# Where the inverse of a softmax row sum is taken: GpSimd's power operation or VectorE's reciprocal

## The reference

```
xn  = layernorm(x)
q,k,v = xn @ Wq + bq, xn @ Wk + bk, xn @ Wv + bv        (16 heads of 128; q as a reshape of the projection)
w   = softmax(q k^T / sqrt(128) + causal mask)
out = x + (w v) @ Wo + bo + ffn(xn)
```

## Time and profile before

| | us |
|---|---|
| median of 3 runs | 1319.09 (1319.01 to 1320.17) |
| profiled execution, its own time | 1319.28 |
| its span, first to last instruction | 1317.0 |
| TensorE busy | 1232.1 (94%) |
| TensorE weight load busy | 1072.9 (81%) |
| VectorE busy | 947.8 (72%) |
| GpSimd busy | 795.8 (60%) |
| ScalarE busy | 766.3 (58%) |

### The profile page before, as it was taken

One profiled execution on the slowest core, in us unless ns is written; L12 is line 12 of the kernel. 1 busy time (PEld: TensorE's weight loads), 2 busy tenths in 40 slices (PEclk: granted clock), 3 DMA queues, 4 the chain that ended last, 5 costly groups with the idle time before them and its releaser, 6 DMA issues.

```text
span 1317.0 us, 20858 instructions
## 1 busy us (share of the span) xinstructions
PE 1232.1 (94%) x7468; PEld 1072.9 (81%) x7468; DVE 947.8 (72%) x1734; ACT 766.3 (58%) x1575; POOL 795.8 (60%) x799
## 2 busy tenths in 40 slices
PE   3799999999899999999999999999999999999997
PEld 2677777777678888888888988898888878889886
DVE  7778877888676667676766677767666776667666
ACT  3565555555446656644666665466665636566653
POOL 5566666666447667644766655366766526666662
PEclk9899999999999999999999999999999999999999
DMA  4000000010210000020000001100000110000012
GB/s 94 12 13 13 13 6 12 12 28 5 57 36 21 15 15 22 13 60 22 21 13 13 25 5 53 33 25 5 21 13 14 40 33 13 13 25 5 13 50 83
DMA packets 60986, 32.43 MB, mean 25 GB/s; under 512 B 17120, under 2 KB 60896, under 8 KB 60896
## 3 DMA queue, kind: packets, MB, share of 16 engines
q1 hardware_dynamic: 59280, 29.99, 8.1%
q10 hardware_dynamic: 1616, 1.25, 0.3%
HBM read 29.12 MB, written 2.10 MB: 24 GB/s over the span
## 4 chain that ended last, share of the span: by engine, by line
PE 52%; DVE 11%; ACT 8%; issue 1%; POOL 1%; DMA 0%; DVEq 0%; SPq 0%; ACTq 0%
PE ps L43 15%; PE ps L45 15%; PE ps L44 15%; PE ps L1079 7%; DVE probs L962 3%; ACT probs L763 3%; DVE pt_lo L916 2%; ACT pt_hi L749 2%; DVE o_lo L921 2%; DVE v_lo L876 1%; DVE q_all L904 1%; ACT o_hi L756 1%; ACT v_hi L720 1%; DVE wq_lo L889 1%; DVE acc L883 0%
## 5 line engine op out<-in xcount | busy, mean ns | idle before, releaser
L916 DVE TENSOR_TENSOR pt_lo<-ps,pt_hi 128x512 fp32r<-128x512 f32 (+3 forms) x384 | 204.4, 553 | 217.9 <-ACT pt_hi L749 215.1
L845 POOL TENSOR_TENSOR inv_sum<-row_sum,minus_one 128x1 f32<-128x1 f32 x256 | 141.5, 553 | 295.8 <-ACT probs L763 295.8
L848 POOL TENSOR_TENSOR probs<-probs,inv_sum 128x128 f32<-128x128 f32 (+7 forms) x256 | 296.4, 1158 | 20.1
L763 ACT ACTIVATE probs<-probs,neg_max 128x128 f32<-128x128 f32 (+7 forms) x256 | 198.5, 775 | 144.3 <-DVE neg_max L962 141.6
L749 ACT ACTIVATE pt_hi<-ps 128x512 fp32r<-128x512 f32 (+3 forms) x384 | 173.8, 488 | 93.3 <-PE ps L1079 90.4
L962 DVE CUSTOM_DVE_ANT_0 probs<-ps,mask_row 128x128 f32<-128x128 f32 (+7 forms) x256 | 192.1, 751 | 3.4 <-PE ps L45 0.7
L1079 PE MATMUL ps<-ident,probs 128*128 128x128 f32 x1152 | 172.3, 277 | 9.1 <-DVE pt_lo L916 8.4
L44 PE MATMUL ps<-pt_lo,v_hi 128*128 128x256 f32 (+1 forms) x640 | 177.5, 277 | 0.0
L45 PE MATMUL ps<-pt_hi,v_lo 128*128 128x256 f32 (+1 forms) x640 | 177.2, 277 | 0.0
L43 PE MATMUL ps<-pt_hi,v_hi 128*128 128x256 f32 (+1 forms) x640 | 170.7, 267 | 0.7 <-DVE pt_lo L916 0.7
L269 POOL TENSOR_TENSOR hid_lo<-hid,hid_hi 128x512 fp32r<-128x512 f32 x64 | 83.1, 1298 | 104.8 <-ACT hid_hi L328 104.8
(11 more groups left out here) (109 smaller groups left out, 3006.1 us busy)
## 6 DMA issues: line engine op xcount, KB each, us to landing
wq_in<-in_wq SPq DMA_DIRECT2D x64, 128.0 KB, 2.3
kv_in<-in_wk SPq DMA_DIRECT2D x16, 256.0 KB, 2.7
kv_in<-in_wv SPq DMA_DIRECT2D x32, 128.0 KB, 2.3
wo_in<-in_wo SPq DMA_DIRECT2D x32, 128.0 KB, 2.0
q_all<-in_x SPq DMA_DIRECT2D x1, 2048.0 KB, 9.5
out<-q_all SPq DMA_DIRECT2D x8, 256.0 KB, 2.2
raw<-in_gate SPq DMA_DIRECT2D x18, 64.0 KB, 1.8
raw<-in_up SPq DMA_DIRECT2D x18, 64.0 KB, 2.0
```

Of the source, the lines that this page charges most:

```text
L763: nc.scalar.activation(probs[:, s % 4, 0:width], probs[:, s % 4, 0:width], ACT.Exp, bias=neg_max[:, s % 16:s % 16 + 1], scale=-1.0, accum_ ...
L845: nc.gpsimd.tensor_tensor(inv_sum[:, at], row_sum[:, at], minus_one[:], ALU.pow).then_inc(inv_done, 1)
L848: nc.gpsimd.tensor_tensor(row, row, inv_sum[:, at].to_broadcast([P, (i + 1) * P]), ALU.mult).then_inc(probs_done, 1)
L916: nc.vector.tensor_tensor(pt_lo[where], T[at % 2][:, 0:blocks * P].rearrange("p (a b) -> p a b", b=P), pt_hi[where].bitcast(F32), ALU.subt ...
```

## The change

The power operation on GpSimd is gone. VectorE takes the reciprocal of the row sum of tile s - 1, directly behind the maximum of tile s; it waits for the exp of tile s - 1. The last tile's reciprocal stands after the loop, ahead of the last `pt_low` calls. GpSimd waits for `inv_done`, now counted up by VectorE, before it multiplies.

```diff
             for s in range(NH * TILES):
                 h, i = divmod(s, TILES)
                 at = slice(s % 16, s % 16 + 1)
-                pool.wait_ge(exp_done, s + 1)
-                nc.gpsimd.tensor_tensor(inv_sum[:, at], row_sum[:, at], minus_one[:], ALU.pow).then_inc(inv_done, 1)
                 pool.wait_ge(inv_done, s + 1)
                 row = probs[:, s % 4, 0:(i + 1) * P]
...
+            def reciprocal(s):
+
+                at = slice(s % 16, s % 16 + 1)
+                dve.wait_ge(exp_done, s + 1)
+                nc.vector.reciprocal(inv_sum[:, at], row_sum[:, at]).then_inc(inv_done, 1)
...
                     -1.0, -MASKED, ALU.add, ALU.min, neg_max[:, s % 16:s % 16 + 1]).then_inc(max_done, 1)
+                if s > 0:
+                    reciprocal(s - 1)
                 if not hurry:
                     evacuate(job_of(h, EARLY_AT.get(i)))
...
             end = NH * TILES
+            reciprocal(end - 1)
             pt_lows(end - 3)
```

## The result

The changed kernel takes 1339.84 us (median of 4 runs, 1337.95 to 1340.40) against 1319.55 us for the kernel before, run beside it: ratio 1.0151, 95% interval 1.0133 to 1.0169. It is slower by 20.3 us; forecast were 14.8 (1333.9 us, range 1329 to 1340). A second time, beside the later experiments, it took 1340.30 us, ratio 1.0143 (1.0127 to 1.0160). The profiled execution took 1337.95 us, its span 1335.7, 18.7 us more than before.

The account below looks back on a forecast made before the run. TensorE's own work plus two short wait loops (`v_lo`, `pt_lo`) was taken to bound the kernel. 27 x 0.53 = 14.3 us plus 0.5 for the first and last head gave 14.8, hence 1333.9 us, range 1329 to 1340.

Parts of the forecast that it names:

- The stall of tile 3: Tile 3's inverse must wait for the maximum of tile 4, so TensorE's transposes stand 0.53 us in 27 heads, 14.3 us.
- The reciprocal's duration: Each reciprocal on VectorE was taken as 0.17 us, from the nearest row `var_eps`, with bounds 0.08 and 0.281 us.
- The estimate from the table of 58 cycles: A reciprocal on VectorE takes about 0.06 us, making each stall 0.11 us shorter and the whole 3.0 us less.
- The rival in which GpSimd holds it: Tile 2's reciprocal in odd heads is held by GpSimd's `vw_lo`, adding 2.5 us: 1336.4 us; 7 in 100.
- Neither wait shrinks: TensorE's waits for `v_lo` (27 times, 8.6 us) and `pt_lo` (30 times, 8.2 us) stay as long as before.
- Tile 4 adds nothing: Tile 4's transposes, possible at 656.26, stand at 656.34 after tile 3's stall; 0.08 us is left, nothing added.
- The failed step: In the three heads preparing new queries, four query steps on TensorE cover tile 3's delay, so these heads cost nothing.
- VectorE's added work costs nothing: 256 reciprocals add at most 43.5 us busy time on VectorE, mostly in idle places; at worst 0.01 us at tile 2.
- The gain in head 0 is taken back: Without the power operation tiles 1 and 2 of head 0 come earlier, but tile 3 waits for tile 4's maximum.
- First and last head: These heads have another order; each was given between 0 and 0.53 us, taken as 0.25, together 0.5 us.
- The upper end: Top of the range: start at 652.66, reciprocal 0.28 us, stall 0.72 us x 29 = 20.9 us, giving 1340.0 us.
- the forecast's own path: The delay from the next tile's maximum through reciprocal and multiplication to tile 3's transposes: 14.8 us in all, 1333.9 us.

Follow-up runs that it names:

- experiment 1: Kernel before, GpSimd's power operation kept but made to wait also for the next tile's maximum, nothing added on VectorE: 1368.46 us, ratio 1.0368.
- experiment 3: Changed kernel with tile 3's reciprocal moved from behind the maximum of tile 4 to ahead of the low part of tile 1: 1332.55 us, ratio 1.0103.
- experiment 6: Changed kernel with tile 3's reciprocal ahead of the low part of tile 1 and tile 4's ahead of the maximum of tile 5: 1325.22 us, ratio 1.0039.
- experiment 4: Changed kernel with the next head's `q_lo` put ahead of the multiplication of tile 6 on GpSimd in heads 7, 15 and 23: 1337.20 us, ratio 1.0131.
- experiment 5: Changed kernel with `wo_lo` put ahead of the multiplication of tile 2 on GpSimd in heads 7, 15 and 23: 1336.93 us, ratio 1.0129.
- experiment 2: Kernel before plus 256 reciprocals on VectorE in the change's places, written to an unread spare tile; GpSimd's power kept: 1321.81 us, ratio 1.0020.
- experiment 7: Changed kernel with each reciprocal moved to the first place meant to follow its exp, and `wo_lo` early in heads 7, 15, 23: 1320.10 us, ratio 0.9997.

## Why the prediction was right, and what it missed

- **The stall of tile 3: right, step by step.** Start of the reciprocal with the accumulator read (657.35 both), duration 0.16 us where I took 0.17, hand-over to GpSimd 657.59 - 657.51 = 0.08, multiplication 1.04, hand-over to TensorE 658.69 - 658.63 = 0.06. Stall 0.52 us for 0.53, 27 times for 27. Over the 27 heads the transposes fall back by 0.50 us at tile 3 and 0.02 at tile 4. Experiments 1, 3 and 6 show that it hangs on the date.
- **The reciprocal's duration.** Over 256 instructions it is 0.156 us at least, 0.158 in the median and 0.185 at most. The estimate from the table of 58 cycles in the Trainium skill, "VectorE: DVE Perf Modes", section on the TRN2 errata, 0.06 us, does not hold here; the 150 cycles that the same section reports as measured (0.16 us) do. The rival in which GpSimd holds it falls: 45 of the 256 ran wholly while GpSimd was in an instruction, 12 of them at tile 2 of odd heads beside `vw_lo`, and the longest of these took 0.164 us.
- **"Neither wait shrinks": right in the ordinary heads.** There both old waits of TensorE are as long as before. The wait for `pt_lo` was to stay at 30 times and came 27 times, 7.6 us for 8.2: in the three heads with new queries it vanished behind the wait for `q_lo`, and experiment 4 brings it back.
- **Tile 4 adds nothing: right as long as tile 3 stalls.** The 0.08 us that I left it depended on the stall. Without it tile 4 is 0.26 us late, as experiment 3 shows. My own dates would have said so: with no reciprocal of tile 3 ahead of the maximum of tile 5, they give 656.09 for transposes that stood at 655.81, 0.28 us.
- **The failed step: "In the three heads that prepare new queries, four query steps of twelve matmuls each stand on TensorE between that maximum and these transposes; they cost nothing."** At tile 3 that is so (0.03 us at most), but the heads cost 4.9 us in two other places, tile 2 and tile 6. I followed the date of the multiplied tile to its transposes and left out what stands behind the multiplication in GpSimd's queue: `q_lo` behind tile 6, awaited by the next head's scores, and `wo_lo` behind tile 2, awaited by a load on SyncE with the query weights' loads behind it. Experiments 4 and 5 show one each.
- **VectorE's added work costs nothing: right for the changed kernel.** VectorE idled for exp ahead of two of the 256 reciprocals only, 0.03 us and, at the very last tile, 1.24 us. By itself the added work costs 2.4 us (experiment 2). Standing in front of the stall or in idle places it costs none (experiments 6 and 7).
- **The gain in head 0 is taken back: right in part.** In the changed kernel tiles 1 and 2 of head 0 come 0.7 to 0.9 us earlier relative to tile 0, and at tile 3 TensorE waits 0.78 us. By tile 7 the head is still 0.5 us ahead of before in the first profile of the changed kernel, and 0.1 us in the second.
- **First and last head, 0.5 us in my sum:** the last one lost 0.3. Head 0, as just said, differs between two profiles by 0.4 us.

The account against the forecast of 14.8: 14.0 for 14.3 from the ordinary heads, 0.3 for 0.5 at the ends, and 4.9 for 0 in the heads with new queries. The sum is 19.2 us, the span grew by 18.7; the 0.5 us between them lie ahead of tile 7 of head 0. The median of the runs lies 1.6 us above this; the last section shows a cause of that size that comes and goes between runs, though that it acts here is not shown.

That 1339.84 us lies inside the range, 0.2 us below its upper end of 1340.0, is luck. The upper end stood for a reciprocal of 0.28 us and a stall of 0.72 us in 29 heads. The reciprocal took 0.16 and the stall 0.52, and with these the forecast's own path gives about 1334 us; the rest came from a path that the forecast had left at nothing. The second measurement, 1340.30, lies just above the range. What was right is the direction, the stall of tile 3, its size and its number.

## What to carry to other kernels

A producer moved to another engine inherits the place it is given in that engine's queue: write down the earliest time at which its inputs are there and the time at which its turn comes, and follow the later one to everybody behind it. That includes the small instructions queued behind its consumer and the transfers waiting for those; the profile's slack of the main consumer says nothing about them. When a stall is removed, look again at the neighbours, for a shorter one may have stood in its shadow.

## What the runs showed that I had not expected

TensorE's clock after a wait differs between executions with the same order of work. Near the end TensorE waits 2.0 us for `o_lo`, then goes on with an output job and transposes. The views are stretches of 4 us of the work behind this wait, first in the kernel before, then in the repeated run of the changed kernel (columns: stretch, length, busy time of each engine, granted clock, DMA).

```profile
1297.00:1301.00 4.00, 4.00 (x30) 3.69 (x31) 3.62 (x7) 0.98 (x2) 0.23 (x1) 1.00 0.38 131
```

```profile
1317.00:1321.00 4.00, 3.86 (x16) 3.51 (x17) 3.10 (x6) 1.09 (x2) 0.21 (x1) 0.59 0.38 131
```

A mean of 1.00 is the 2.4 GHz level all through; 0.59 is the 1.2 GHz level for most of the stretch. In the same 4 us TensorE's records are 30 and 16. The order of work there is the same, and so is the wait ahead of it (2.01 and 2.02 us). Of the ten profiles of this document five show the lower clock there, 0.57 to 0.66 over the 4 us from the end of this wait (experiments 2, 4, 5, 7 and the repeated run), and five 1.00. In nine of them the wait is 2.00 to 2.03 us, in experiment 1 it is 1.65 us (clock 1.00). Between two profiles of the changed kernel it moved the transposes of the last tile by 1.5 us. A step of this size is about half of the spread of the kernel before, 1318.4 to 1321.9 us; that it makes that spread is not shown, as only one of those runs was profiled. The first stage varies as well: the first transposes start between 380.7 and 382.9 us in the ten profiles. So single profiles of this kernel are not to be compared closer than about 2 us over the whole span, only place by place. What decides between the two clocks stays open.
